# Opening of an attention and feed-forward kernel: constant-tile matmuls during the first loads, bias columns straight from DRAM, x of the first group in halves

## The chip, the cores and the metric

The kernel runs on one core of one Trainium2 chip. The metric is the device time of one execution in microseconds (us), lower is better. A run gives several executions; the profile is that of one.

## The reference, cut to what matters

x is 2 x 4096 x 256, float32. One causal attention layer and one routed feed-forward layer, each followed by a layer norm:

```python
qkv = x @ w_attn + b_attn                       # 256 -> 768
attn = softmax(q @ k.T / sqrt(256) + causal_mask)
x = layernorm(x + (attn @ v) @ w_proj + b_proj)
scores = x @ w_router                            # top 3072 of 4096 rows of a batch
x = layernorm(where(row is among the top, gelu(x @ w_block), x) + x)
```

## The kernel before, in words

The 8192 rows are cut into 16 groups G of 512 rows, 8 for each batch. A group's queries are projected, multiplied with the keys of all its earlier tiles, put through a softmax and multiplied with the values; then come the output, the norm and the feed-forward part. Projection matrices are folded. A = Wq Wk^T serves for the scores, so that "q" is x A plus a column `ucol`, and x itself plays the keys. WV = Wv Wp (less its last column) serves for the values. Every float32 operand of a large product is held as a high part (rounded, written by ScalarE) and a low part (the rest, written by VectorE or GpSimd), and `split3` makes three matmuls of each pair.

The start is the function `prepare`. TensorE makes, in the program's order:
- `columns` (L562): six matmuls of one column that turn the row `b_row` of biases into columns in PSUM, copied to `bcols` (L603).
- `product` (L554): wq times wk, from which VectorE makes A's high and low part (`a_parts`, L597 and L599).
- `sums` (L569, L572, L575): ten matmuls of one column with the biases (`ucol`, the last column of WV, `bqbk`).
- then `pe_q` of group 0 (L498 into fbank from A and xT), twice six matmuls of 512 columns;
- `values_weights` (L580) and `bias` (L586, L587), from which VectorE makes WV (`w_parts`, L615 to L625) and `b_tot`;
- `scores` of group 0 (L498 into sbank), `pe_v` of group 0 (L498 into fbank from WV), and the row maxima (`row_max`, L871 and L892).

In the trace a plain float32 matmul shows as two records (a product's four matmuls are 8 records); L498's are one record each.

x of group 0 goes from DRAM into `xraw` (L667), is rounded by ScalarE (`xhi`, L687) and its low part comes from VectorE for the first 128 channels (`first_xlo`, L696) and from GpSimd for the others (L692). `block_parts` and `router_sum` (L636 to L644) make the feed-forward weights' parts and wait for the loads of w_block and w_router.

The order on each engine is written out ahead of time. Every operation belongs to a named stream of its engine; a planner (`planned`) steps through estimated costs and start times and takes, among the streams' next operations, the one that can start first. `MARGIN_US` makes a stream look later, `PREFER_US` decides between those that can start at once, `COLD_US` is until when TensorE's work is costed at `COLD` = 1.85 times, and `DMA_BYTES_US` is the rate of a load. The engines then run these orders strictly, with semaphore waits. SP issues all DMAs, in its own order. In front of GpSimd's planned order stand the memsets of the constants.

Of the kernel before, what the change touches and what calls it, by code (L numbers as in the profile page):

```python
# [16 lines left out]
P = 128  # L17
# [25 lines left out]
LATE = 2 * (T // GQ) - 2  # L43

# [12 lines left out]
MARGIN_US = {"attention_out router": 3, "project xhi": 2, "final scale": 1.5, "out": 1, "final result": 1,  # L57
             "row_max reduce": 1, "scores hide": 1, "final_roots": 0.6, "values load": 0.6, "ffn aggr": 0.6,
             "project load": 0.3, "proj": 0.3, "ffn flo": 0.3}
# [5 lines left out]
class Rehearsal:  # L65
# [27 lines left out]
    def matmul(self, out, lhs, rhs, start, stop):  # L93
        passes = 4 if rhs.dtype == F32 else 1
        self.time += max(.06, .0132 + self.per_element * passes * out.shape[-1])
        return self
# [96 lines left out]
def planned(todo, signalled, urgent):  # L193
# [23 lines left out]
    for _ in range(sum(len(m) for s in todo.values() for m in s.values())):  # L217
# [28 lines left out]
        if r.bytes:  # L246
            dma = max(when + DMA_US, dma) + r.bytes / DMA_BYTES_US
# [23 lines left out]
def program(nc, x, xt, w_attn_t, b_attn, w_proj, b_proj, w_router, w_block, out):  # L271
# [61 lines left out]
    with ctx:  # L333
# [74 lines left out]
        b_row = ring[0:1, STAGED + 6:STAGED + 8, :].rearrange("p n c -> p (n c)")[:, 0:3 * C]  # L408
# [12 lines left out]
        ld_xt0 = [sem(f"ld_xt0_{n}") for n in range(EARLY + 1)]  # L421
        ld_x = [sem("ld_x0"), sem("ld_x1")]
# [6 lines left out]
        p_a, p_bcols, p_u, p_w, p_btot = sem("p_a"), sem("p_bcols"), sem("p_u"), sem("p_w"), sem("p_btot")  # L429
# [64 lines left out]
        def split3(eng, o, lhs, rhs, chunks):  # L494

            todo = [(lh, rh, k) for k in range(chunks) for lh, rh in ((0, 0), (0, 1), (1, 0))]
            for n, (lh, rh, k) in enumerate(todo):
                mm = eng.matmul(o, lhs(lh, k), rhs(rh, k), start=n == 0, stop=n == len(todo) - 1)  # L498
            return mm
# [25 lines left out]

        def prepare():
# [6 lines left out]
            def load_b(sp):  # L533
                sp.dma_start(b_row, b_attn.rearrange("(a c) -> a c", a=1)).then_inc(ld_b, 16)

            def load_w(sp):
                sp.dma_start(wv_t, wt_rows[2]).then_inc(ld_w, 16)
                sp.dma_start(wp, w_proj.rearrange("(k p) c -> p k c", p=P)).then_inc(ld_w, 16)
                sp.dma_start(bp_row, b_proj.rearrange("(a c) -> a c", a=1)).then_inc(ld_w, 16)

            def load_block(sp):
                sp.dma_start(wb, w_block.rearrange("(k p) c -> p k c", p=P)).then_inc(ld_ffw, 16)
                sp.dma_start(wr[:, :], w_router.rearrange("(a c) -> a c", a=1).broadcast_to([P, C])).then_inc(ld_ffw, 16)
            at("sp", "prepare", load_b)
            at("sp", "prepare", load_qk)
            project_load(0)
# [11 lines left out]
            def columns(pe):  # L558
                pe.wait_ge(ld_b, 16)
                pe.wait_ge(g_const, 1)  # L560
                for n in range(3 * CC):
                    mm = pe.matmul(small[:, n:n + 1], b_row[:, n * P:(n + 1) * P], one_row[:, 0:1], start=True, stop=True)  # L562
                mm.then_inc(p_bcols, 1)

            def sums(pe):
                pe.wait_ge(v_bcols, 2)
                for m in range(CC):
                    for k in range(CC):
                        pe.matmul(small[:, 8 + m:9 + m], wk_t[:, k, m * P:(m + 1) * P], bcols[:, 0, k:k + 1], start=k == 0,  # L569
                                  stop=k == CC - 1)  # L570
                    for k in range(CC):
                        pe.matmul(small[:, 10 + m:11 + m], wq_t[:, k, m * P:(m + 1) * P], bcols[:, 1, k:k + 1],  # L572
                                  start=k == 0, stop=k == CC - 1)
# [4 lines left out]
            def values_weights(pe, m, k):  # L578
                pe.wait_ge(ld_w, 16 * 3)
# [3 lines left out]
            def bias(pe):  # L583
                pe.wait_ge(v_bcols, 3)
# [3 lines left out]
            for op in (columns, product, sums):  # L588
                at("pe", "prepare", op)
            pe_fill["values weights"] = [lambda pe, m=m, k=k: values_weights(pe, m, k) for m in range(CC) for k in range(CC)] + [bias]  # L590
# [10 lines left out]
            def bias_columns(dve):  # L601
                dve.wait_ge(p_bcols, 1)
                dve.tensor_copy(bcols[:, :, :].rearrange("p s k -> p (s k)"), small[:, 0:3 * CC]).then_inc(v_bcols, 1)  # L603
                dve.wait_ge(v_bcols, 1)
# [3 lines left out]
            def bias_sums(dve):  # L608
                dve.wait_ge(p_u, 1)
                dve.tensor_copy(ucol[:, :], small[:, 8:8 + CC]).then_inc(v_u, 1)  # L610
                dve.tensor_copy(bqbk[:, :], small[:, 12:13]).then_inc(v_u, 1)

            def w_parts(dve):
# [6 lines left out]
                dve.wait_ge(p_u, 1)  # L620
                dve.tensor_copy(w_diff[:, :, LAST], small[:, 10:10 + CC]).then_inc(v_wdiff, 1)
                dve.wait_ge(v_wdiff, 2)
                dve.tensor_copy(WV[:, 0], w_diff).then_inc(v_wv, 1)
                dve.wait_ge(v_wv, 1)
# [15 lines left out]
            for op in (bias_columns, bias_sums):  # L640
                at("dve", "prepare bias", op)
# [3 lines left out]
            at("dve", "prepare late", w_parts)  # L645
# [13 lines left out]
        def project_load(G):  # L659
            b, g = groups[G]  # L660

            def load(sp):
                if G == EARLY + 1:
# [4 lines left out]
            at("sp", "project load" if G else "prepare", load)  # L668

        def project(G):  # L670
# [17 lines left out]
            at("act", "project xhi", xhi)  # L688

            def xlo(pool, k):  # L690
                pool.wait_ge(a_xhi, G + 1)
                pool.tensor_tensor(xT[:, 1, k, cols], raw_of(G)[:, k, :], f32(xT[:, 0, k, cols]), ALU.subtract).then_inc(g_xlo, 1)  # L692

            def first_xlo(dve):
                dve.wait_ge(a_xhi, 1)
                dve.tensor_tensor(xT[:, 1, 0, cols], xraw[:, 0, :], f32(xT[:, 0, 0, cols]), ALU.subtract).then_inc(v_xlo, 1)  # L696
            if G == 0:
                at("dve", "prepare xlo", first_xlo)
            for k in range(1 if G == 0 else 0, CC):
                at("pool", "project xlo", lambda pool, k=k: xlo(pool, k))  # L700

            def pe_q(pe, m):
                xlo_made(pe, G)
                if G == 0:
                    pe.wait_ge(v_a, 2)
                freed(pe, ("q", G, m))
                split3(pe, bank_of(("q", G, m))[:, :], lambda h, k: A[:, h, k, m * P:(m + 1) * P],
                       lambda h, k: xT[:, h, k, cols], CC).then_inc(p_proj, 1)
# [268 lines left out]
        def attention_out(G):  # L977
# [5 lines left out]
            def load(sp):  # L983
                if G >= 2:
# [3 lines left out]
                    filled(sp, ("ft", G - 2, 1))  # L988
                sp.dma_start(r, x_rows[b][:, tile0:tile0 + QT, :]).then_inc(ld_x[G % 2], 16)
# [597 lines left out]
        def _(pool):  # L1587

            pool.memset(ones[:, :], 1.0).then_inc(g_const, 1)
# [3 lines left out]
            pool.memset(ones_bf[:, :], 1.0).then_inc(g_const, 1)  # L1593
# [64 lines left out]
```

## Time and profile before

| | us |
|---|---|
| median of 3 runs (990.3 to 991.2) | 990.65 |
| profiled execution | 990.68 |
| its span in the trace | 988.9 |
| TensorE busy | 943.7 |
| VectorE busy | 771.7 |
| ScalarE busy | 637.6 |
| GpSimd busy | 280.0 |

The span runs from the first to the last instruction; 1.8 us of the profiled execution lie outside it. PE is TensorE's matmuls, PEld its weight loads, DVE VectorE, ACT ScalarE, POOL GpSimd, SPq the DMA issues of SyncE. Busy time is a sum over stages: TensorE is nearly always busy from 50 us to 940 us, and has pauses at both ends.

### The profile page before, as it was taken

Reading aid. Unit: us, or ns where it says so; the run is one execution under the profiler, and the core shown is the slowest. Engines: PE = TensorE matmul, PEld = TensorE weight load, DVE = VectorE, ACT = ScalarE, POOL = GpSimd, SP = SyncE. Lnnn points to the kernel's source line nnn. Section 1 sums busy time; section 2 is a strip of 40 time slices with the busy share of each in tenths; the row PEclk is TensorE's granted clock in tenths of the full one; section 3 lists DMA queues with packets and bytes.
Section 4 is the critical chain, followed back from the end, with each engine's and each line's share of the span. In section 5 each row is a group of like instructions: output and inputs, shape, how many; then the busy total and the mean of one; then the engine's idle time right before and its main releaser. Section 6 shows DMA issues by size and latency. Waiting matters only on the chain.

```text
span 988.9 us, 15341 instructions
## 1 busy us (share of the span) xinstructions
PE 943.7 (95%) x4922; PEld 804.9 (81%) x4922; DVE 771.7 (78%) x1475; ACT 637.6 (64%) x1005; POOL 280.0 (28%) x426
## 2 busy tenths in 40 slices
PE   7899999999999999999999999999999999998972
PEld 6788888888888888888888888888788888887851
DVE  4689697966876695679698889888799779469977
ACT  3557576663873595567667757585688558348983
POOL 5421235141041024513343332212101502121323
PEclk9999999999999999999999999999999999999975
DMA  5542445343353336558533334335777434337915
GB/s 195 199 135 75 118 129 160 107 139 107 96 153 114 96 107 188 160 184 267 169 118 118 117 125 142 118 106 190 240 228 241 137 107 123 122 96 242 344 53 171
DMA packets 88948, 149.26 MB, mean 151 GB/s; under 512 B 7586, under 2 KB 25379, under 8 KB 88868
## 3 DMA queue, kind: packets, MB, share of 16 engines
q1 hardware_dynamic: 88868, 148.28, 47.3%
q8 instruction: 40, 0.66, 0.3%
q14 instruction: 40, 0.33, 0.1%
HBM read 108.40 MB, written 39.85 MB: 150 GB/s over the span
## 4 chain that ended last, share of the span: by engine, by line
PE 87%; DVE 4%; ACT 3%; DMA 2%; issue 2%; POOL 1%; DVEq 0%; SPq 0%; ACTq 0%
PE sbank L498 36%; PE fbank L498 12%; PE obank L955 11%; PE obank L957 11%; PE obank L956 11%; DMA xraw<-xt 2%; PE fbank L1034 1%; PE fbank L1174 1%; PE mbank L871 1%; DVE tail L1528 1%; PE mbank L892 1%; ACT parts L916 1%; ACT ring L909 1%; ACT tail L1518 1%; DVE runmax L833 1%
## 5 line engine op out<-in xcount | busy, mean ns | idle before, releaser
L498 PE MATMUL sbank<-qT,xT 128*128 128x512 f32 (+2 forms) x1728 | 410.4, 378 | 4.2 <-issue 2.2
L498 PEld LDWEIGHTS sbank<-qT,xT 128*128 128x128 f32 x1728 | 305.9, 188 | 58.8 <-issue 3.7
L796 ACT COPY ring<-sbank 128x512 f32<-128x512 f32 (+3 forms) x288 | 157.6, 549 | 174.9 <-PE sbank L498 120.1
L955 PE MATMUL obank<-ring_lo,vs 128*128 128x512 f32 (+3 forms) x576 | 219.1, 380 | 3.2 <-ACT ot_sb L1006 1.6
L957 PE MATMUL obank<-parts,vs 128*128 128x512 f32 (+3 forms) x576 | 216.5, 376 | 0.0
L956 PE MATMUL obank<-parts,vs 128*128 128x512 f32 (+3 forms) x576 | 216.3, 376 | 0.0
L921 DVE TENSOR_TENSOR ring_lo<-ring,parts 128x1024 fp32r<-128x1024 f32 (+4 forms) x176 | 176.2, 1011 | 34.3 <-ACT parts L916 33.4
L902 DVE TENSOR_TENSOR ring<-ring,mbank 128x1024 f32<-128x1024 f32 (+4 forms) x176 | 159.8, 949 | 11.1 <-PE mbank L892 11.1
L916 ACT CAST parts<-ring 128x1024 fp32r<-128x1024 f32 (+4 forms) x176 | 145.4, 833 | 34.1 <-PE obank L957 33.6
L838 DVE TENSOR_TENSOR runmax<-ring,runmax 128x1024 f32<-128x1024 f32 x84 | 108.5, 1292 | 69.9 <-ACT ring L796 69.4
L909 ACT ACTIVATE ring<-ring 128x1024 f32<-128x1024 f32 (+4 forms) x176 | 143.5, 844 | 25.3 <-DVE ring L902 25.0
L955 PEld LDWEIGHTS obank<-ring_lo,vs 128*128 128x128 f32 x576 | 108.7, 189 | 21.6 <-ACT parts L916 3.3
L957 PEld LDWEIGHTS obank<-parts,vs 128*128 128x128 f32 x576 | 108.6, 188 | 19.6
L956 PEld LDWEIGHTS obank<-parts,vs 128*128 128x128 f32 x576 | 108.8, 189 | 18.0
L1219 POOL TENSOR_TENSOR yb<-xres,yb 128x512 f32<-128x512 f32 x28 | 36.4, 1321 | 295.2 <-ACT yb L1210 295.2
L998 POOL TENSOR_TENSOR xres<-xres,b_tot 128x512 f32<-128x512 f32 x32 | 50.2, 1591 | 69.8 <-DMA xres<-x 64.8
L692 POOL TENSOR_TENSOR xT<-xraw,xT 128x512 fp32r<-128x512 f32 x27 | 39.1, 1468 | 51.7 <-ACT xT L687 51.7
L498 PE MATMUL fbank<-WV,xT 128*128 128x256 f32 x384 | 51.3, 283 | 1.7 <-DVE WV L625 1.7
L498 PE MATMUL fbank<-xT,A 128*128 128x512 f32 x192 | 51.0, 403 | 1.8 <-DVE A L599 0.9
L498 PEld LDWEIGHTS fbank<-WV,xT 128*128 128x128 f32 x384 | 49.5, 191 | 3.9 <-DVE WV L625 2.2
L833 DVE TENSOR_TENSOR runmax<-ring,runmax 128x512 f32<-128x512 f32 (+3 forms) x76 | 41.7, 548 | 13.5 <-ACT ring L796 11.8
L970 POOL TENSOR_SCALAR roots<-mv_h 128x4 f32<-128x4 f32 x15 | 8.0, 532 | 144.8 <-DVE mv_h L1057 144.8
(190 smaller groups left out, 1013.0 us busy)
## 6 DMA issues: line engine op xcount, KB each, us to landing
vs<-v_scratch SPq DMA_DIRECT2D x288, 256.0 KB, 2.7
v_scratch<-vnew SPq DMA_DIRECT2D x30, 512.0 KB, 3.1
xres<-x SPq DMA_DIRECT2D x16, 512.0 KB, 4.0
out<-tail SPq DMA_DIRECT2D x32, 256.0 KB, 3.3
xraw<-xt SPq DMA_DIRECT2D x14, 512.0 KB, 4.2
x_scratch<-xres SPq DMA_DIRECT2D x14, 512.0 KB, 3.1
y_scratch<-yb SPq DMA_DIRECT2D x14, 512.0 KB, 3.9
tail<-x_scratch SPq DMA_DIRECT2D x28, 256.0 KB, 3.2
```

The costliest lines, as they stand in the source:

```text
L498: mm = eng.matmul(o, lhs(lh, k), rhs(rh, k), start=n == 0, stop=n == len(todo) - 1)
L796: act.copy(slot(n)[:, c0:], sbank[n % NSS][:, c0:]).then_inc(a_copy, 1)
L833: dve.tensor_tensor(runmax[:, 0, c0:], slot(n)[:, c0:], runmax[:, 0, c0:], ALU.max).then_inc(v_max, 1)
L838: dve.tensor_tensor(runmax[:, :, :], slots(ns, 0), runmax[:, :, :], ALU.max).then_inc(v_max, 1)
L902: dve.tensor_tensor(slots(ns, c0), slots(ns, c0), mbank[:, None, c0:].broadcast_to([P, len(ns), GQ - c0]), ALU.subtract).then_inc(v_z, 1)
L909: act.activation(slots(ns, c0), slots(ns, c0), ACT.Exp, scale=SCALE).then_inc(a_exp, 1)
L916: act.copy(hi_of(u), slots(ns, c0)).then_inc(a_hi, 1)
L921: dve.tensor_tensor(slots_lo(ns, c0), slots(ns, c0), f32(hi_of(u)), ALU.subtract).then_inc(v_lo, 1)
L955: pe.matmul(o, vh, lo_, start=i == 0, stop=False)
L956: pe.matmul(o, vh, hi_, start=False, stop=False)
L957: mm = pe.matmul(o, vl, hi_, start=False, stop=last)
L998: pool.tensor_tensor(r[:, 2 * j:2 * j + 2], r[:, 2 * j:2 * j + 2], b_tot[:, None, :].broadcast_to([P, 2, C]), ALU.add).then_inc(g_xres, 1)
```

## The change

- `WARM` = 8 matmuls of `ones_bf` (128 x 128) with 512 columns of the same tile, bfloat16, into obank[1], as TensorE's first work. GpSimd sets `ones_bf` first.
- `columns` and its copy are gone: the host hands b_attn over as 128 x 6, and one DMA puts it into `bcols`. `sums` is cut in three: `key_sums` behind `product`, `query_sums` and `bias_product` behind `values_weights`.
- SP's order at the start: wq, wk, x of group 0 in two halves of 128 channels (256 KB each, their own semaphores), then b_attn. The loads of wv, wp, b_proj wait until the first half of x has landed; those of x of groups 1 and 2 and of the residual's x of groups 0 and 1 wait until wv has landed.
- `first_xhi` rounds the halves one by one. GpSimd makes the low part of half 0, VectorE that of half 1; the wait for the latter stands in front of the fourth matmul of the first query product.
- `block_parts` and `router_sum` stand behind the two `qlo` of group 0 in the stream "project qlo". `w_parts` is cut in three operations.
- The planner's numbers: `COLD_US` 21 to 4, a first load rate, a longer least time of a plain float32 matmul, and many entries of `PREFER_US` and `MARGIN_US`. They bear on the orders of the whole program.

The diff, cut to its core:

```diff
+WARM = 8
-DMA_US, DMA_BYTES_US = 1.6, 320e3
+DMA_US, DMA_BYTES_US, FIRST_BYTES_US = 1.6, 320e3, 250e3
-COLD_US, COLD, COLD_STREAMS = 21.0, 1.85, ("late", "last")
+COLD_US, COLD, COLD_STREAMS = 4.0, 1.85, ("late", "last")
-PREFER_US = {"attention_out stats": 60, "row_max reduce": 60, "project qhi": 60, "scores copy": 30,
-             "softmax hi": 30, "row_max": 8, "scores hide": 8, "project vlo": 8, "softmax lo": 4, "ffn gelu": 4,
-             "ffn aggr": -8, "attention_out router": -8, "final pick": -15, "attention_out score": -30,
-             "softmax z": -30, "project vhi": -30}
+PREFER_US = {"ffn flo": 100, "row_max reduce": 60, "project qhi": 60, "attention_out residual": 60,
+             "project qlo": 60, "attention_out stats": 30, "scores copy": 30, "softmax hi": 30, "final_roots": 30,
+             "row_max": 8, "scores hide": 8, "prepare xlo": 8, "project xhi": 8, "project vlo": 4,
+             "softmax lo": 4, "ffn gelu": 4, "softmax exp": -4, "ffn aggr": -8, "attention_out router": -8,
+             "project vhi": -8, "final pick": -15, "attention_out score": -30, "softmax z": -30,
+             "final result": -30}
...
             def load_b(sp):
-                sp.dma_start(b_row, b_attn.rearrange("(a c) -> a c", a=1)).then_inc(ld_b, 16)
+                sp.dma_start(bcols[:, :, :].rearrange("p s k -> p (s k)"), b_attn).then_inc(ld_b, 16)
+            def load_x(sp, k):
+                sp.dma_start(xraw[:, k, :], xt_rows[0][:, k, 0:GQ]).then_inc(ld_xh[k], 16)
             def load_w(sp):
-                sp.dma_start(wv_t, wt_rows[2]).then_inc(ld_w, 16)
+                sp.wait_ge(ld_xh[0], 16)
+                sp.dma_start(wv_t, wt_rows[2]).then_inc(ld_wv, 16)
...
-            at("sp", "prepare", load_b)
             at("sp", "prepare", load_qk)
-            project_load(0)
+            for k in range(CC):
+                at("sp", "prepare", lambda sp, k=k: load_x(sp, k))
+            at("sp", "prepare", load_b)
             at("sp", "prepare", load_w)
...
+            def warm(pe):
+                pe.wait_ge(g_const, 1)
+                for _ in range(WARM):
+                    pe.matmul(obank[1][:, :].rearrange("p (a b) -> p a b", a=QT), ones_bf[:, :],
+                              ones_bf[:, None, :].broadcast_to([P, QT, P]), start=True, stop=True)
-            for op in (columns, product, sums):
+            for op in (warm, product, key_sums):
                 at("pe", "prepare", op)
+            pe_fill["values weights"] += [lambda pe, m=m: query_sums(pe, m) for m in range(CC)] + [bias_product, bias]
...
             for op in (block_parts, router_sum):
-                at("dve", "prepare block", op)
+                after_queries.append(op)
...
             def load(sp):
+                if G <= EARLY:
+                    sp.wait_ge(ld_wv, 16)
...
+            def first_xhi(act, k):
+                act.wait_ge(ld_xh[k], 16)
+                act.copy(xT[:, 0, k, cols], xraw[:, k, :]).then_inc(a_xhi if k else a_xh0, 1)
...
             def pe_q(pe, m):
-                xlo_made(pe, G)
                 if G == 0:
                     pe.wait_ge(v_a, 2)
+                    pe.wait_ge(g_xlo, 1)
+                else:
+                    xlo_made(pe, G)
                 freed(pe, ("q", G, m))
                 split3(pe, bank_of(("q", G, m))[:, :], lambda h, k: A[:, h, k, m * P:(m + 1) * P],
-                       lambda h, k: xT[:, h, k, cols], CC).then_inc(p_proj, 1)
+                       lambda h, k: xT[:, h, k, cols], CC,
+                       between=(lambda: pe.wait_ge(v_xlo, 1)) if G == 0 and m == 0 else None).then_inc(p_proj, 1)
...
             project(G)
+            if not G:
+                for op in after_queries:
+                    at("dve", "project qlo", op)
```

## Rows read from the trace of the kernel before

**Rows 1.** The page: busy time and share of each engine
```profile
PE 943.7 (95%) x4922; PEld 804.9 (81%) x4922; DVE 771.7 (78%) x1475; ACT 637.6 (64%) x1005; POOL 280.0 (28%) x426
```

**Rows 2.** Stretches: busy time by engine, granted clock, DMA share, GB/s
```profile
0.00:50.00 50.00, 40.82 (x212) 34.81 (x213) 28.64 (x59) 20.37 (x34) 24.55 (x48) 0.97 0.59 197
50.00:940.00 890.00, 880.98 (x4594) 752.89 (x4593) 707.16 (x1295) 588.59 (x912) 241.50 (x349) 1.00 0.48 151
940.00:988.90 48.90, 21.92 (x120) 17.23 (x118) 35.90 (x122) 28.68 (x61) 13.94 (x30) 0.64 0.32 110
```

**Rows 3.** Timeline of PE: start, us, line, instructions, idle before
```profile
2.21 2.71 PE L562 MATMUL mbank<-ones,ring 1*128 1x1 f32 x12 [2.21 <-DMA ring<-b_attn]
4.85 3.41 PE L554 MATMUL sbank<-ring 128*128 128x256 f32 x8
...
11.33 4.50 PE L498 MATMUL fbank<-xT,A 128*128 128x512 f32 x12 [0.94 <-DVE A L599]
15.66 1.89 PE L580 MATMUL obank<-ring 128*128 128x256 f32 x8
...
18.35 0.69 PE L587 MATMUL obank<-ring,ones 1*128 1x256 f32 x2
19.72 1.63 PE L498 MATMUL sbank<-qT,xT 128*128 128x512 f32 x6 [0.68 <-issue]
23.08 3.14 PE L498 MATMUL fbank<-WV,xT 128*128 128x256 f32 x24 [1.74 <-DVE WV L625]
...
28.35 0.89 PE L498 MATMUL sbank<-qT,xT 128*128 128x128 f32 x6 [0.37 <-ACT ring L796]
```

**Rows 4.** Short stretches of the start, same columns as rows 2
```profile
4.85:8.10 3.25, 3.25 (x9) 2.67 (x9) 0.95 (x3) 0.06 (x1) 0.69 (x11) 1.00 0.88 272
8.10:10.40 2.30, 2.29 (x21) 2.20 (x19) 1.28 (x6) 0.99 (x1) 1.23 (x1) 1.00 1.04 384
11.30:15.70 4.40, 4.37 (x13) 3.51 (x14) 0.01 (x1) 2.32 (x3) 3.73 (x4) 0.63 0.99 338
...
29.20:36.40 7.20, 3.96 (x21) 2.74 (x21) 5.45 (x12) 2.83 (x5) 2.19 (x3) 1.00 0.85 292
```

**Rows 5.** Timeline of SP: DMA issues
```profile
0.79 0.35 SPq L534 DMA_DIRECT2D ring<-b_attn  x1
1.19 0.90 SPq L531 DMA_DIRECT2D ring<-w_attn_t  x2
2.14 0.47 SPq L667 DMA_DIRECT2D xraw<-xt  x1
```

**Rows 6.** The view of DMAs: issues, KB each, median us to landing
```profile
ring<-w_attn_t SPq DMA_DIRECT2D x3, 256.0 KB, 3.0
```

**Rows 7.** Timeline of the other engines at the start
```profile
0.78 0.20 POOL L1589 MEMSET ones<- 128x128 f32 x1 [0.29 <-POOLq L1651]
...
8.04 1.04 ACT L687 CAST xT<-xraw 128x1024 fp32r<-128x1024 f32 x1 [5.98 <-DMA xraw<-xt]
...
9.12 0.69 DVE L696 TENSOR_TENSOR xT<-xraw,xT 128x512 fp32r<-128x512 f32 x1 [3.18 <-ACT xT L687]
9.17 1.76 POOL L692 TENSOR_TENSOR xT<-xraw,xT 128x512 fp32r<-128x512 f32 x1 [3.57 <-ACT xT L687]
...
10.49 0.69 DVE L599 TENSOR_TENSOR A<-sbank,A 128x512 fp32r<-128x512 f32 x1
...
15.92 1.33 DVE L636 CAST WB<-ring 128x512 fp32r<-128x512 f32 x1 [4.61 <-DMA wr<-w_router]
...
21.40 1.63 DVE L625 TENSOR_TENSOR WV<-ring,WV 128x512 fp32r<-128x512 f32 x1
```

**Rows 8.** The chain that ended last, start and us
```profile
11.03 7.62 DMA xraw<-xt
...
22.51 3.85 DMA xraw<-xt
```

**Rows 9.** A stretch late in the program, columns of rows 2
```profile
710.00:720.00 10.00, 7.12 (x28) 5.41 (x27) 6.72 (x12) 6.84 (x12) 0.09 (x1) 0.89 0.76 250
```

More of the change, by code:

```diff
@@ L94, in matmul @@
         passes = 4 if rhs.dtype == F32 else 1
-        self.time += max(.06, .0132 + self.per_element * passes * out.shape[-1])
+        self.time += max(.22 if passes == 4 else .06, .0132 + self.per_element * passes * int(np.prod(out.shape[1:])))
         return self
@@ L246, in planned @@
         if r.bytes:
-            dma = max(when + DMA_US, dma) + r.bytes / DMA_BYTES_US
+            dma = max(when + DMA_US, dma) + r.bytes / (DMA_BYTES_US if when > 10 else FIRST_BYTES_US)
         for t, name, by in r.incs:
@@ L524, in program @@
         w_psum = obank[1][:, :].rearrange("p (m c) -> p m c", m=CC)
+        after_queries = []
         def prepare():
@@ L556, in product, with key_sums, query_sums, bias_product @@
                 mm.then_inc(p_a, 1)
-            def columns(pe):
+            def key_sums(pe):
                 pe.wait_ge(ld_b, 16)
[L560 to L566, printed above, removed]
                 for m in range(CC):
                     for k in range(CC):
[L569 to L573, printed above, removed]
+                        mm = pe.matmul(small[:, 8 + m:9 + m], wk_t[:, k, m * P:(m + 1) * P], bcols[:, 0, k:k + 1],
+                                       start=k == 0, stop=k == CC - 1)
+                mm.then_inc(p_u, 1)
+            def query_sums(pe, m):
+                pe.wait_ge(v_u, 1)
+                for k in range(CC):
+                    mm = pe.matmul(small[:, 10 + m:11 + m], wq_t[:, k, m * P:(m + 1) * P], bcols[:, 1, k:k + 1],
+                                   start=k == 0, stop=k == CC - 1)
+                mm.then_inc(p_u, 1)
+            def bias_product(pe):
+                pe.wait_ge(v_bcols, 1)
                 for k in range(CC):
@@ L587, in bias @@
                 pe.matmul(obank[0][:, 0:C], one_row, bp_row, start=False, stop=True).then_inc(p_btot, 1)
-            for op in (columns, product, sums):
+            def warm(pe):
[4 more added lines that the diff above has]
+            for op in (warm, product, key_sums):
                 at("pe", "prepare", op)
-            pe_fill["values weights"] = [lambda pe, m=m, k=k: values_weights(pe, m, k) for m in range(CC) for k in range(CC)] + [bias]
+            pe_fill["values weights"] = [lambda pe, m=m, k=k: values_weights(pe, m, k) for m in range(CC) for k in range(CC)]
+            pe_fill["values weights"] += [lambda pe, m=m: query_sums(pe, m) for m in range(CC)] + [bias_product, bias]
             def a_parts(dve):
@@ L639, in prepare @@
             at("dve", "prepare", a_parts)
-            for op in (bias_columns, bias_sums):
+            at("dve", "prepare keys", key_bias)
+            for op in (bias_columns, row_bias):
                 at("dve", "prepare bias", op)
@@ L687, in xhi @@
                 act.copy(xT[:, 0, :, cols], raw_of(G)).then_inc(a_xhi, 1)
-            at("act", "project xhi", xhi)
+            def first_xhi(act, k):
+                act.wait_ge(ld_xh[k], 16)
+                act.copy(xT[:, 0, k, cols], xraw[:, k, :]).then_inc(a_xhi if k else a_xh0, 1)
+            if G:
+                at("act", "project xhi", xhi)
+            else:
+                for k in range(CC):
+                    at("act", "project xhi", lambda act, k=k: first_xhi(act, k))
             def xlo(pool, k):
-                pool.wait_ge(a_xhi, G + 1)
+                if G:
+                    pool.wait_ge(a_xhi, G + 1)
+                else:
+                    pool.wait_ge(a_xh0, 1)
                 pool.tensor_tensor(xT[:, 1, k, cols], raw_of(G)[:, k, :], f32(xT[:, 0, k, cols]), ALU.subtract).then_inc(g_xlo, 1)
@@ L988, in load @@
                     filled(sp, ("ft", G - 2, 1))
+                else:
+                    sp.wait_ge(ld_wv, 16)
                 sp.dma_start(r, x_rows[b][:, tile0:tile0 + QT, :]).then_inc(ld_x[G % 2], 16)
@@ L1587, in _ @@
         def _(pool):
+            pool.memset(ones_bf[:, :], 1.0).then_inc(g_const, 1)
             pool.memset(ones[:, :], 1.0).then_inc(g_const, 1)
```

48 lines of the change are left out of this document (27 added, 21 removed).

## The prediction

> **What bounds the kernel now.** I read the page's busy shares first: TensorE 95%, VectorE 78% [rows 1]. The reader is to see that no other engine comes near. The table by stretches says where the missing 5% are: from 50 to 940 us TensorE is busy 881.0 of 890 us, in the first 50 us it is 40.8, and in the last 48.9 us 21.9 [rows 2]. The middle is TensorE's own work, which the edit leaves as it is, so whatever brings the middle forward comes off the end, and nothing else at the start does. The last stretch is VectorE's (35.9 of 48.9 us) and its matmuls run at a mean granted clock of 0.64; the edit touches it only through the planner's orders.
>
> So I read the start instruction by instruction on TensorE [rows 3]. It is in a chain there: biases land, `columns`, `product` from 4.85, sums, a pause of 0.94 us for A's low part, queries at 11.33, a pause of 0.68 us before the first scores, 1.74 us before v, 0.37 us at 28.35, and then 7.2 us of which 3.96 are busy [rows 4].
>
> Two stretches run slowly. The product's 8 records take 3.41 us; the same 8 records of the same shape take 1.89 us at 15.66 [rows 3]. That is the ratio of TensorE's two levels, 1.2 and 2.4 GHz, though the clock column reads 1.00 at 4.85 [rows 4]; it seems to show changes only, so at the very start I trust the durations. The queries' 12 matmuls take 4.50 us with 0.63 granted in the stretch [rows 3, 4]; the six score matmuls of the same 512 columns at 19.72 take 1.63 us. Twelve at full clock are then 2.9 us (0.24 each and the last one's latency).
>
> **The first operands.** Before, b_attn's issue stood first (0.79), wq and wk followed at 1.19 and 1.64, the latter landing 3.0 us after its issue, about 4.65 [rows 5, 6]. Now the two issues are 0.40 us earlier: 4.25. The warm matmuls begin when GpSimd's first memset is done, 0.78 + 0.20 = 0.98 us [rows 7]. The trace has no bfloat16 matmul of 512 columns; the nearest are float32r ones of one pass, 0.375 each in the mixed queries and about 0.48 at half clock, so 3.0 to 3.8 us for eight. They end between 4.0 and 4.8; I take 4.6 (nearer the half-clock row, since the engine comes from rest). They can hold the product by up to 0.55 us; beside them `columns` (2.71 us) goes, whose work was hidden before the product anyhow: nothing gained, nothing lost. The product starts at 4.6 instead of 4.85.
>
> At what clock? After 2.7 us of one-column matmuls and 3.4 us of product the sums run fast (20 records in 2.3 us, 0.115 each), so steady activity from 2.2 to 8 had raised it; with dense matmuls from 1 us on I take the product at full clock: 1.9 us, end 6.5 (at half clock 8.0, the upper bound).
>
> The Trainium skill, TensorE: Matmul & The Clock Gate, "What's actually happening", says the same from the other side: rest is the half-rate state, activity releases it, idling gives it back. By its first half the eight matmuls do their work; by its second half the clock could be lost again in the wait ahead of the queries, as it was at 11.33; that outcome is priced as a rival below from the rows alone.
>
> **x and the biases.** x of group 0 was issued at 2.14 and reached ScalarE at 8.04, 5.9 us later, with wv, wp and x of group 1 behind it in the same queue and 272 GB/s moved meanwhile [rows 4, 5, 7]. Now it is issued at 1.7 and 2.15 and nothing but 3 KB follows until half 0 has landed. 512 KB at 272 GB/s are 1.9 us, after wk's 4.25: half 0 at 5.2, half 1 at 6.2. The other end is no gain but the earlier issue: 7.6. ScalarE rounds a half in 0.55 us (1.04 for both): done at 5.8 and 6.8. GpSimd's low part costs up to 1.76: 7.6. VectorE's costs 0.69 and is wanted only by the fourth matmul.
>
> The bias columns are 128 rows of 24 bytes. No row prices this alone; the row of 3 KB landed in time for a start at 2.21, 1.4 us after issue, and here they queue behind x, so 6.3 (up to 7.7, x's upper end). `key_sums` are 8 records: 0.9 us, 6.5 to 7.4 (8.6).
>
> The Trainium skill, DMA: Bandwidth & Descriptors, "Specifications", speaks against such rows: runs under 512 bytes are below the size for line rate and cost a read-modify-write. With 128 of them it would add little even so; no row here shows it, and the sum goes by the bounds above.
>
> A's parts on VectorE: 6.56, two of 0.69, 7.95. So all three inputs of the queries meet at 7.6 to 8.0, and I take 8.0 for their start: **3.3 us earlier** (with x at its upper end and half a clock, 9.3: 2.0 earlier). At full clock they take 2.9 for 4.5 us: **1.6 us**.
>
> **From the queries to the end of group 0's scores.** The pause of 0.68 us goes: VectorE's `qlo` was then queued behind WB's high part, which sat 4.61 us waiting for w_router [rows 7]; it now comes first, and TensorE has the values' weights to do from 10.9 to 15.7. The pause of 1.74 goes too if WV is ready before TensorE has done the rest: it needs p_w, about 12.8, the last column (14.3), the two parts, 0.7 and up to 1.63, so about 17; with block_parts' 2.4 us in front, 20. TensorE's other work (values' weights and bias 15.66 to 19.04, i.e. 3.4; the moved sums 1.4; scores about 4, by 1.63 for the 512 columns at 19.72 and less for 384, 256 and 128) lasts until about 19.7, so at worst 0.3 us of it stays. **2.4 us**. The 0.37 at 28.35 stays. The moved sums are 12 records of 0.115: they were ahead of the queries and now lie on the path behind them, **1.4 us lost**.
>
> Costed at nothing: the second half's own DMA issue (0.45 us of SP) and the waits that now stand ahead of wv's and the later x loads. Queued on SP behind them are w_block, w_router, the residual's x and the x of groups 1 and 2: wv goes out at 5.2, the others when it has landed, about 3 us later, at 8.2. Group 1's x, 512 KB behind wp at some 340 GB/s [rows 4], lands at 11 to 13, and its queries, which came after 28.35 + 0.89, are wanted at about 23. That cover is 10 us; without it the delay would be paid in full. The stretch 29.2 to 36.4 with 3.2 us of pauses is the maxima's chain and I leave it alone (1.5 either way).
>
> **The sum.** -3.3 - 1.6 - 2.4 + 1.4 = -5.9 us on the profiled 990.68, that is 984.8; the median of the runs is 0.03 from it, so 984.8 stands for that too. The changed preferences reorder all engines everywhere. In the middle TensorE has 9 us of pauses to win or lose [rows 2]; I take 0, and 2 us for the gain's end.
>
> **Rivals.**
> - **Half clock all the same** (0.15): the product at 3.4 us and the queries at 4.5 cost 1.5 + 1.6 back: -2.8, 987.9. For it: the clock was lost at 11.33 after a stretch of full PE rows [rows 4], and `key_sums` are as thin. Against: they last 0.9 us, not 2.3.
> - **The loads did not move** (0.17): x of group 3 lands at 18.65 and that of group 4 at 26.36 [rows 8], the first 7.6 us after its issue, behind the other loads in the queue, the second behind group 3's low part. Neither gets 6 us earlier. If an engine's order has the rounding of such an x (or the wait for w_router) ahead of v's evacuation, as now at 26.4, TensorE stands there again. About 3.4 us are given back: 988.2.
> - **Hidden anyway** (0.08): the maxima's chain of group 0 and the first value loads set the date of the middle; 990 to 990.7.
> - **Slower** (0.10): the new orders make one kind of gap more often. At 710 us TensorE is 2.88 us idle, waiting for scores copied late, and the clock falls to 0.89 over 10 us, 1.1 more: 4.0 us a gap [rows 9]. One more leaves 988.8; two end at 992.8. It decides from 7.9 us given back, two gaps; two at the batches' joints would be enough. Against it: in 890 us there is 9 us of pause in all.
>
> The forecast has the remaining 0.50. Its own range is 982.0 to 987.0: reorder gain of 2 us and a later meeting of product and x. Faster by over 0.2% (below 988.7, about what a measurement of this kernel can tell from no change) holds the forecast, half clock, and three quarters of the second rival: 0.77. Within 0.2%: the rest of it, the third, one gap of the fourth: 0.15. Slower: 0.08. The range of 8 in 10 is 981.8 to 989.6: from the bounds' best to the case that one gap or late loads leave 1 us.
>
> **What would show it.** TensorE's queries of group 0 at 8.0 (before 11.33) and in 2.9 us; the product's 8 records in 1.9 us; the first scores at about 15.7 (before 19.72); v of group 0 without a pause over 0.5 us; group 0's last scores (before 28.35) at about 22.5; in the table by stretches 50 to 940 us with the same 9 us of pauses. Wrong would be: 0.5 granted after 8 us; a wait of ScalarE for x of group 3 or 4 ahead of v; VectorE waiting for w_router; TensorE's pauses from 50 us on over 12 us; an end stretch longer than 48.9 us.

## The result and the profile after

| | before | changed |
|---|---|---|
| median of 4 runs, us | 990.92 | 982.74 |
| lowest to highest, us | 990.3 to 991.56 | 982.11 to 984.62 |
| profiled execution, us | 990.68 | 982.49 |
| its span, us | 988.9 | 980.8 |

The ratio of the changed kernel's time to before's is 0.9926, 95% interval 0.9911 to 0.9942: faster by 8.2 us in the medians where 5.9 were forecast, and inside the range of 981.8 to 989.6. Between the profiled executions it is 8.19 us.

The page's busy shares of the changed kernel answer to [rows 1], its stretches to [rows 2] (the cut at 932 keeps the end stretch at the same length):

```profile
PE 941.2 (96%) x4918; PEld 800.3 (82%) x4918; DVE 774.7 (79%) x1474; ACT 638.5 (65%) x1006; POOL 279.4 (28%) x426
```

```profile
0.00:50.00 50.00, 43.42 (x232) 35.10 (x232) 35.41 (x64) 22.54 (x38) 25.33 (x48) 1.00 0.59 197
50.00:932.00 882.00, 875.98 (x4565) 748.24 (x4566) 703.36 (x1289) 586.37 (x907) 239.51 (x346) 1.00 0.48 152
932.00:980.80 48.80, 21.82 (x123) 16.97 (x121) 35.89 (x122) 29.55 (x63) 14.51 (x33) 0.68 0.33 109
```

TensorE has 6.0 us of pauses between 50 and 932 us, before 9.0 between 50 and 940. The end stretch is as long as it was, and TensorE and VectorE are as busy in it.

The changed kernel's timeline of TensorE, against [rows 3] (start, us, line, instructions, idle before):

```profile
1.04 3.53 PE L608 MATMUL obank<-ones_bf 128*128 128x512 bf16 x8 [1.04 <-POOL ones_bf L1639]
4.41 1.90 PE L568 MATMUL sbank<-ring 128*128 128x256 f32 x8
6.35 1.05 PE L576 MATMUL mbank<-bcols,ring 128*128 128x1 f32 x8
7.82 3.01 PE L503 MATMUL fbank<-xT,A 128*128 128x512 f32 x12 [0.41 <-DVE A L622]
...
15.31 2.72 PE L503 MATMUL sbank<-qT,xT 128*128 128x512 f32 x12
18.60 3.13 PE L503 MATMUL fbank<-WV,xT 128*128 128x256 f32 x24 [0.57 <-DVE WV L653]
...
24.44 1.61 PE L503 MATMUL fbank<-xT,A 128*128 128x512 f32 x6 [1.38 <-DVE row_const L805]
...
27.70 1.61 PE L503 MATMUL fbank<-xT,A 128*128 128x512 f32 x6 [1.22 <-DVE qT L766]
...
31.23 1.62 PE L503 MATMUL sbank<-qT,xT 128*128 128x512 f32 x6 [1.49 <-issue]
```

The product's 8 records take 1.90 us (before 3.41), the queries start at 7.82 (11.33) and take 3.01 (4.50), the scores follow at 15.31 (19.72), v at 18.60 (23.08). Then two pauses for VectorE stand that were not there, 1.38 and 1.22 us; the one of 1.76 before the row-max transposes (32.43 before) is gone, that of 1.49 before group 1's scores stays. The other engines of the changed kernel, against [rows 7]:

```profile
5.42 1.36 ACT L722 CAST xT<-xraw 128x512 fp32r<-128x512 f32 x2 [3.35 <-DMA xraw<-xt]
...
6.12 1.27 POOL L734 TENSOR_TENSOR xT<-xraw,xT 128x512 fp32r<-128x512 f32 x1 [0.52 <-ACT xT L722]
...
7.07 0.69 DVE L622 TENSOR_TENSOR A<-sbank,A 128x512 fp32r<-128x512 f32 x1
...
12.80 0.43 DVE L664 CAST WB<-ring 128x512 fp32r<-128x512 f32 x1 [0.46 <-DMA wr<-w_router]
...
16.88 1.66 DVE L653 TENSOR_TENSOR WV<-ring,WV 128x512 fp32r<-128x512 f32 x1
```

ScalarE's first rounding starts at 5.42, not 8.04; it is for half 0 and half 1. A's low part ends last, as forecast. VectorE is at WB from 12.80, and WV's low part ends at 18.54, which is when v starts.

To see where the 8.2 us arise, I cut the executions at four matmuls found in every kernel, and take the distances. M1 is the start of group 1's row-max transposes (55.57 before), M2 a later transpose with a pause of 0.24 us (494.79), M3 the value matmul behind a pause of 1.41 us (904.16), M4 the first feed-forward matmul after the last group's values (943.77). The numbers come from TensorE's timelines.

| us | to M1 | M1 to M2 | M2 to M3 | M3 to M4 | M4 to the end |
|---|---|---|---|---|---|
| before | 55.57 | 439.22 | 409.37 | 39.61 | 45.13 |
| changed | 50.37 | 439.40 | 404.74 | 42.01 | 44.28 |
| difference | -5.2 | +0.2 | -4.6 | +2.4 | -0.9 |

The start gives 5.2 us. Nearly as much again, 4.6, comes between M2 and M3, and half of that is lost behind M3. The pause of 2.35 us at 717 (in the stretch of [rows 9], 2.88 idle and 0.89 granted) is gone, and so is one of 1.09 at 542.

### The profile page after: what moved, and what is told of

Read it like the earlier page. It is cut to its first block, busy times and chain, and to the rows that moved or that the text cites. A ratio compares the mean times of both kernels' runs of the same rounds, so it can differ in the third digit from the quotient of the medians.

```text
span 980.8 us, 15337 instructions
## 1 busy us (share of the span) xinstructions
PE 941.2 (96%) x4918; PEld 800.3 (82%) x4918; DVE 774.7 (79%) x1474; ACT 638.5 (65%) x1006; POOL 279.4 (28%) x426
## 4 chain that ended last, share of the span: by engine, by line
PE 82%; DVE 6%; ACT 4%; issue 3%; DMA 2%; SPq 0%; POOL 0%; DVEq 0%; ACTq 0%
PE sbank L503 35%; PE fbank L503 11%; PE obank L1000 11%; PE obank L1002 11%; PE obank L1001 11%; PE fbank L1221 1%; PE fbank L1081 1%; ACT parts L961 1%; ACT ring L954 1%; DMA out<-tail 1%; DVE tail L1575 1%; PE mbank L916 1%; DMA tail<-y_scratch 1%; DVE runmax L878 1%; PE mbank L937 1%
## 5 line engine op out<-in xcount | busy, mean ns | idle before, releaser
L966 DVE TENSOR_TENSOR ring_lo<-ring,parts 128x1024 fp32r<-128x1024 f32 (+4 forms) x176 | 178.9, 1024 | 31.7 <-ACT parts L961 30.4
L878 DVE TENSOR_TENSOR runmax<-ring,runmax 128x512 f32<-128x512 f32 (+3 forms) x76 | 43.7, 575 | 12.8 <-ACT ring L841 11.1
```

Of the source, the lines that this page charges most:

```text
L878: dve.tensor_tensor(runmax[:, 0, c0:], slot(n)[:, c0:], runmax[:, 0, c0:], ALU.max).then_inc(v_max, 1)
L966: dve.tensor_tensor(slots_lo(ns, c0), slots(ns, c0), f32(hi_of(u)), ALU.subtract).then_inc(v_lo, 1)
```

## The experiments

Each kernel was timed in five rounds beside the kernel before. I give the median time, its ratio to the kernel before with the 95% interval, and M1. Each experiment has one profile, so its M1 is that of one execution.

**Preferences alone.** The kernel before with the changed `PREFER_US` and `MARGIN_US`:

```diff
-PREFER_US = {"attention_out stats": 60, "row_max reduce": 60, ...
+PREFER_US = {"ffn flo": 100, "row_max reduce": 60, ...
-MARGIN_US = {"attention_out router": 3, "project xhi": 2, "final scale": 1.5, ...
+MARGIN_US = {"attention_out router": 3, "final scale": 3, "project xhi": 2, ...
...
```

> The kernel before with only the changed PREFER_US and MARGIN_US. Theory A (the change is two separate gains: about 5.2 us at the start from the loads, the clock and the moved sums, and about 3 us later from the planner's preferences): group 1's row-max transposes stay at 55 to 56 us as before, the gap at 717 us is gone, the time is 986 to 989. Theory B (the later 3 us are chance of where the start's shift lets waits fall): the time is 990 to 992 with the gap at 717 us or one like it. Theory C (the preferences also make the start): transposes of group 1 earlier than 54.

987.16 us, 0.9967 (0.9953 to 0.9982). M1 is at 55.40, as before; M2 to M3 is 404.97, the changed kernel's; M4 to the end is 46.54, that is 1.4 more. The longest wait of TensorE for VectorE between 60 and 930 us in this kernel (total, times, longest):

```profile
PE mbank L873 <- DVE runmax L835: 1.4, 1, 1.4
```

It was 2.4 us at 717 in the kernel before, with the clock's fall behind it; here the clock stays at 1.00 from 700 to 730 us. A pause of 1.37 us at 714 is what is left of it, and the one of 1.09 at 542 is gone. Theory A: the preferences are worth 3 us (medians: 2.9) without any change of M1. Its queries are the slowest of all:

```profile
12.67 5.30 PE L500 MATMUL fbank<-xT,A 128*128 128x512 f32 x12
```

They end at 17.97, 2.1 us later than before (15.83), and M1 is no later. What stands ahead of v on TensorE does not by itself set M1; v waits for VectorE's WV in both kernels.

**All but the preferences.** The changed kernel with the two tables of before:

```diff
-PREFER_US = {"ffn flo": 100, "row_max reduce": 60, ...
+PREFER_US = {"attention_out stats": 60, "row_max reduce": 60, ...
...
```

> The changed kernel with the PREFER_US and MARGIN_US of before; all else as changed. Theory A: group 1's row-max transposes within 0.7 us of the changed kernel's 50.37, a gap of 2 us or more with a fall of the clock between 500 and 890 us, time 985 to 987. Theory B: time within 1 us of the changed kernel's or anywhere else between 981 and 988, not tied to such a gap. Theory C: transposes of group 1 later than 52.

985.19 us, 0.9954 (0.9942 to 0.9966). M1 is at 52.05 and M2 to M3 406.97, which lies between both; there is no gap of 2 us (the largest at that place are 0.97 at 711 and 1.34 at 735) and no fall of the clock between 50 and 940, so theory A is right in the sum and not in the place. Its start:

```profile
4.43 2.90 PE L566 MATMUL sbank<-ring 128*128 128x256 f32 x8
...
9.79 2.50 PE L501 MATMUL fbank<-xT,A 128*128 128x512 f32 x5 [1.67 <-DVE A L620]
```

The product takes 2.90 us after the same eight matmuls. VectorE, in this order, widens the biases before it turns to A (its cast of A at 8.33), so TensorE waits 1.67 us and the queries run slowly. So the order that the preferences make costs the queries a wait. That they have a part in M1 (theory C) is not shown: the changed kernel itself has its M1 at 51.80 in a second profile, below. Relative to the kernel before, this kernel gains 4.8 us and the one above 2.9, together 7.7; the changed kernel itself was 7.7 under before in the series below. The two halves add, as far as such medians tell (the intervals are over 1 us to either side).

**The changed kernel again**, as the measure of the next three.

> The changed kernel as it is, once more, as the measure for the others of this series and to see how much of the start is the same in a second profile. Theory (the product's and the queries' clock at the start is the same in every execution): product's 8 records 1.9 us, queries 3.0 us, group 1's row-max transposes within 0.3 us of 50.37, all times within 1 us. Rival (the clock comes in at another date from execution to execution, as the kernel with the old preferences hints, whose product took 2.90 us after the same eight matmuls): product between 1.9 and 3.4 us and times that spread over 2 us or more.

982.81 us (981.61 to 984.01), 0.9918 (0.9900 to 0.9936). M1 is at 51.80, 1.4 us later than in the first profile; M1 to M2 is 439.34 and M2 to M3 404.94, within 0.2 of the first. TensorE and the others:

```profile
4.43 2.20 PE L568 MATMUL sbank<-ring 128*128 128x256 f32 x8
...
8.19 3.00 PE L503 MATMUL fbank<-xT,A 128*128 128x512 f32 x12 [0.20 <-DVE A L622]
```

```profile
6.07 1.29 ACT L722 CAST xT<-xraw 128x512 fp32r<-128x512 f32 x2 [4.00 <-DMA xraw<-xt]
...
14.79 0.43 DVE L664 CAST WB<-ring 128x512 fp32r<-128x512 f32 x1 [2.09 <-DMA wr<-w_router]
```

The rival holds: the product took 2.20 us, and VectorE waited 2.09 us for w_router where it had waited 0.46. Of the 1.4 us, 0.4 are there when the queries start (8.19 against 7.82) and 0.9 when v does, since WV was made at 19.41 and not at 18.54; the pause for VectorE behind v is 1.87 and not 1.38. Yet the execution lasted 981.61 us, less than the first one: M3 to M4 is 39.66 instead of 42.01. At that place both executions have the same two pauses. Stretches of the first profile of the changed kernel, then of the second:

```profile
710.00:720.00 10.00, 10.00 (x63) 9.00 (x62) 9.35 (x18) 6.55 (x13) 0.00 (x0) 1.00 0.63 201
...
880.00:890.00 10.00, 8.36 (x56) 7.40 (x55) 8.29 (x17) 6.11 (x13) 0.00 (x0) 1.00 0.57 188
890.00:900.00 10.00, 8.47 (x37) 7.07 (x36) 10.00 (x11) 9.83 (x12) 1.31 (x2) 0.83 0.75 246
```

```profile
880.00:890.00 10.00, 8.67 (x62) 7.86 (x60) 7.22 (x15) 5.13 (x11) 0.00 (x0) 1.00 0.42 145
890.00:900.00 10.00, 8.18 (x41) 6.99 (x42) 10.00 (x11) 9.97 (x13) 0.00 (x0) 1.00 0.76 254
```

In the first the clock falls to 0.83 over 10 us after the pauses, in the second it stays. That fall is about 1.6 of the 2.35 us; the rest goes with a pause of 0.46 us at 925 that only the first has (the last section works this out from all profiles). So one execution says little about 2 us.

**No constant-tile matmuls**, orders unchanged (the planner goes on costing them):

```diff
-                for _ in range(WARM):
+                for _ in range(WARM if isinstance(pe, Rehearsal) else 0):
```

> The changed kernel with no constant-tile matmuls; the planner still costs them, so every engine's order is the same. Theory A (they hold the clock up for the product and the queries): the product's 8 records take 3.2 to 3.4 us instead of 1.90, and the queries 3.0 to 4.5; group 1's row-max transposes 1.5 to 3 us later than 50.37, time 984 to 986. Rival (the start is held by loads and by VectorE's queue, so a slow product is absorbed before v): the product is slow but group 1's transposes and the time move by less than 0.7 us.

984.12 us, 0.9933 (0.9918 to 0.9948). M1 at 53.16. TensorE's start:

```profile
4.47 3.75 PE L568 MATMUL sbank<-ring 128*128 128x256 f32 x8 [4.47 <-POOL jtab L1661]
8.02 1.71 PE L576 MATMUL mbank<-bcols,ring 128*128 128x1 f32 x8
```

The product takes 3.75 us and the queries 4.81, both more than I had expected. In the nine profiles with the constant tiles and the same start of the product it takes 3.15 at most. So the constant tiles do give the clock: M1 is 1.4 to 2.8 us later than in the two profiles of the changed kernel. In the time the interval overlaps the changed kernel's, and 1.3 us of medians from two series is no proof.

**The biases as a row again**, in the place of the constant tiles; the bias load is first in the queue again, and the copy of the columns is back:

```diff
-                sp.dma_start(bcols[:, :, :].rearrange("p s k -> p (s k)"), b_attn).then_inc(ld_b, 16)
+                sp.dma_start(b_row, b_line.rearrange("(a c) -> a c", a=1)).then_inc(ld_b, 16)
...
-            for op in (warm, product, key_sums):
+            for op in (columns, product, key_sums):
...
```

> The changed kernel with the biases as a row, turned into columns by six matmuls as before, in the place of the constant-tile matmuls; the bias load is first in the queue again. The prediction's term (these matmuls are hidden ahead of the product; the columns gain nothing but 0.4 us of queue): beside the kernel without constant-tile matmuls, whose product starts at 4.47 and whose group 1 transposes are at 53.16, this one's product starts at 4.8 to 5.0 and its transposes are at 53.0 to 53.8. Rival (the one-column matmuls do warm the clock as well as the constant tile): product in less than 3 us and queries in 3.0 us, transposes near 51.

984.50 us, 0.9934 (0.9916 to 0.9952), M1 at 52.01. The product starts at 5.07 and takes 3.59 us, but the queries, at 10.17, take 3.00. Neither reading is right alone. The one-column matmuls from 2.42 us on do not help the product. That they help the queries is not shown: with the same twelve records from 2.32 us the kernel with the preferences alone had its queries in 5.30 us, and from 2.21 the kernel before in 4.50. The start is no worse than without any matmuls ahead (53.16); the columns by themselves gain nothing that these runs show.

**The loads not held back**, orders unchanged:

```diff
-                sp.wait_ge(ld_xh[0], 16)
+                if isinstance(sp, Rehearsal):
+                    sp.wait_ge(ld_xh[0], 16)
...
-                if G <= EARLY:
+                if G <= EARLY and isinstance(sp, Rehearsal):
                     sp.wait_ge(ld_wv, 16)
...
```

> The changed kernel without the waits that hold back the loads of wv, wp, b_proj until x's first half and of the later x until wv; the planner still counts them, so every order is the same. Theory (x came late because others moved beside it): ScalarE's first rounding at 6.5 to 7.5 us instead of 5.42, the queries at 8.8 to 10 instead of 7.82, but w_router lands earlier and VectorE with it; group 1's row-max transposes between 0.5 and 1.5 us later. Rival (x is short and first in the queue anyway, the waits are worth nothing): rounding before 6, group 1's transposes at 50.4 or earlier.

980.45 us, 0.9895 (0.9875 to 0.9916), M1 at 48.77. In this kernel's timeline:

```profile
6.06 1.31 ACT L723 CAST xT<-xraw 128x512 fp32r<-128x512 f32 x2 [4.00 <-DMA xraw<-xt]
...
12.60 0.42 DVE L665 CAST WB<-ring 128x512 fp32r<-128x512 f32 x1
```

The rival holds, but for 0.06 us in the rounding. x's first half is rounded at 6.06, in the changed kernel's two profiles at 5.42 and 6.07. Over all profiles of x in two loads it is 5.42 to 6.18 with the waits and 5.96 to 6.38 without: what comes behind x in the queue delayed it by no more than it varies. But WB's cast is at 12.60 with no wait, and M1 1.6 to 3.0 us earlier. Once more, beside the combined kernels:

> The kernel without the waits that hold back the loads, once more beside the combined ones. Theory (the waits cost w_router's landing and nothing is won for x): transposes of group 1 within 0.5 us of 48.77, ScalarE's first rounding between 5.4 and 6.2 us as with the waits, time 980 to 981.5, that is 1.5 to 2.5 us under the changed kernel's. Rival (the first profile was a lucky one): transposes at 50 or later, time above 982.

981.78 us, 0.9916 (0.9898 to 0.9932). M1 at 48.88, rounding at 6.15: the start is reproduced. The time is not: M3 to M4 was 42.07 here, with the clock's fall and the pause at 925, and 40.29 in the first, and the median is 1.3 higher. The waits cost the start; that leaving them out makes a faster kernel is not shown.

**The feed-forward weights' parts behind WV:**

```diff
-                after_queries.append(op)
+                at("dve", "prepare late", op)
...
```

> The changed kernel with the feed-forward weights' parts and the router's sum behind the making of WV on VectorE instead of in front of it. Theory (after the queries VectorE's queue is the start's chain: the parts hold it from 12.80 to 14.28 us, WV is done at 18.54 and TensorE stands 0.57, 1.38 and 1.22 us): WV done 1 to 1.5 us earlier, group 1's row-max transposes 1 to 1.5 us earlier than 50.37, time about 981.5 where the later orders are no worse. Rival (the chain is GpSimd's and the loads'): transposes of group 1 within 0.4 us of 50.37.

981.78 us, 0.9915 (0.9901 to 0.9929), M1 at 49.67: 0.7 and 2.1 us before the changed kernel's two. VectorE's timeline of this kernel:

```profile
14.92 0.69 DVE L652 TENSOR_TENSOR WV<-ring,WV 128x512 fp32r<-128x512 f32 x1
...
16.31 0.42 DVE L663 CAST WB<-ring 128x512 fp32r<-128x512 f32 x1
```

WV's low part ends at 15.61, 2.9 us earlier than at 18.54. Of that 0.7 us arrive at M1 of the first profile (2.1 of the second): the planner now has three of the four score products ahead of v, which starts at 19.12 without a pause. M2 to M3 is 406.30, 1.6 more than the changed kernel's. That could be the price of the new orders, but it is not shown. The four kernels that run the changed kernel's own orders with another start (no constant tiles, both without the held-back loads, and x as if in one piece) have 406.07, 406.51, 406.27 and 406.25. So this stretch varies by 1.8 us with the orders as they are, and none of the differences of 2 us in it says what an order is worth.

**Both together**, once with orders planned for it, once with those of the kernel above:

```diff
-                sp.wait_ge(ld_xh[0], 16)
-                if G <= EARLY:
-                    sp.wait_ge(ld_wv, 16)
...
-                after_queries.append(op)
+                at("dve", "prepare late", op)
```

> The changed kernel without the waits that hold back the other loads, as the planner sees it too, and with the feed-forward weights' parts behind WV. Theory (each takes a wait of VectorE's queue off the start: alone 2.0 and 0.7 to 1.4 us): group 1's row-max transposes at 48.3 to 49.3, time 979.5 to 981. Rival (both cure the same wait for w_router, so the second adds nothing, and new orders cost elsewhere): transposes at 48.8 or later, time 980.5 to 982.5.

> The same two edits, but with the orders of the kernel that has only the parts moved (the planner still counts the waits). Theory: start as in the combined kernel, transposes of group 1 at 48.3 to 49.3 us; the time differs from the combined one's only by what 494 to 905 us and the end make of it, under 1.5 us. Rival as for the combined kernel: 48.8 or later.

981.56 us, 0.9911 (0.9886 to 0.9935), M1 at 50.98, after a product of 2.92 us and with the clock at 0.62 from 16 to 20.5 us, where twelve score matmuls took 4.26 us (2.72 in the changed kernel); and 981.69 us, 0.9913 (0.9895 to 0.9932), M1 at 50.02, after wk landed 0.45 us later than elsewhere (product at 4.88). In the times the rival holds: together the edits are no better than either. That both cure the same wait for w_router fits, but these two profiles, each with a late or slow start of its own, do not show it. No kernel here is shown to beat the changed one.

**The query sums ahead of the queries:**

```diff
             for op in (warm, product, key_sums):
                 at("pe", "prepare", op)
+            for m in range(CC):
+                at("pe", "prepare", lambda pe, m=m: query_sums(pe, m))
...
-                dve.wait_ge(p_u, 1)
+                dve.wait_ge(p_u, 1 + CC)
...
```

> The changed kernel with the query sums (8 records of one column) back in front of the queries, the one-column product of the biases left behind. Theory of the prediction (the moved sums lie on the path behind the queries): queries 0.5 us later, what follows 0.4 us earlier, group 1's row-max transposes 0 to 0.5 us earlier. Rival (what holds v is VectorE making WV, and TensorE's sums are hidden in front of it): queries later by 0.4 to 0.9 us, v's start unchanged or later, group 1's transposes 0 to 0.7 us later.

981.77 us, 0.9911 (0.9893 to 0.9929), M1 at 50.47.

```profile
4.43 3.15 PE L568 MATMUL sbank<-ring 128*128 128x256 f32 x8
...
9.11 3.02 PE L503 MATMUL fbank<-xT,A 128*128 128x512 f32 x12
```

Inconclusive. The product took 3.15 us, and the planner moved all scores ahead of v, so that TensorE no longer stood for WV at all. With the queries 0.9 to 1.3 us later, M1 lies between the changed kernel's two.

**x of group 0 as if in one piece:** ScalarE waits for both halves, orders unchanged.

```diff
             def first_xhi(act, k):
+                if not isinstance(act, Rehearsal):
+                    act.wait_ge(ld_xh[1], 16)
```

> The changed kernel, but ScalarE waits for both halves of x before it rounds the first, as if x came in one piece; orders unchanged. Theory (halves matter little, since A's low part ends last before the queries): first rounding 0.6 to 1.0 us later, GpSimd's low part done at 8.5 to 9, queries 0.3 to 1.0 us later, group 1's transposes 0 to 0.7 us later. Rival (the halves carry the start): transposes more than 1 us later than 50.4 to 51.8, the two profiles of the changed kernel.

983.10 us, 0.9924 (0.9903 to 0.9944), M1 at 51.30.

```profile
4.43 2.57 PE L568 MATMUL sbank<-ring 128*128 128x256 f32 x8
...
9.18 3.33 PE L503 MATMUL fbank<-xT,A 128*128 128x512 f32 x7 [1.39 <-POOL xT L736]
```

TensorE waits 1.39 us for GpSimd's low part, and the queries (4.53 us in all) fall to half clock. But the edit did more than it says, as ScalarE's timeline shows:

```profile
5.77 1.28 ACT L724 ACT_TABLE_LOAD   x1 [5.77 <-DMA xraw<-xt]
7.07 1.14 ACT L724 CAST xT<-xraw 128x512 fp32r<-128x512 f32 x2
```

In all other profiles this table load starts at 0.78 or 0.79, while ScalarE has nothing else to do; here the added wait stands ahead of it. Both halves were there at 5.77. Without the 1.28 us GpSimd's low part would end at 7.75 instead of 9.03, A's low part (8.46) would be last, and the queries would start at about 8.5, an estimate from these rows. So nothing here shows that the halves are worth anything. What the run does show is that a start of the queries 1.0 to 1.4 us later, and an end 2.5 to 2.9 us later, need not reach M1, which lies between the changed kernel's two: the pauses of 1.38 and 1.22 us behind v have shrunk to 0.22 and 0.23, with one of 0.76 new between them.

## Why the prediction was right, and where not

- **Bound at the start.** Right. A chain of TensorE, VectorE and the first loads, and what it gives at M1 is there unchanged at M2: M1 to M2 is 439.2 to 439.4 us in all profiles here. But the chain goes by VectorE's WV more than by the queries. With the preferences alone and with x as if in one piece the queries ended over 2 us later and M1 did not.
- **First operands.** Product at 4.6, full clock, 1.9 us: measured 4.41 and 1.90. The eight tiles take 3.53 us, by 4.57 (4.6 forecast). Full clock was one of two bounds and is not certain: after the same tiles the product took from 1.90 to 3.15 us.
- **x.** Half 0 at 5.2: ScalarE starts at 5.42. The reason I gave, that what moved beside it slowed it, is refuted: without the waits x is as early. Its size is not the reason either, as both halves had landed by 7.44 at the latest, and by 5.77 where both are waited for, while the single load of before landed at 8.04. The issue is 0.36 us earlier; what of the rest is due to two loads for one, and what to the biases gone from the front of the queue, no run separates.
- **Queries.** Start at 8.0, 2.9 us: 7.82 and 3.01; 3.3 + 1.6 us forecast, 3.5 + 1.5 found.
- **Pauses behind them.** The pause before the scores went. That for WV fell from 1.74 to 0.57, not to nothing (1.06 in the second profile): WV was done at 18.54, inside my 17 to 20, but the work that was to cover it ended at 18.03 and not at 19.7, since two of the four score products stand behind v. Two pauses for VectorE, 1.38 and 1.22 us, came behind v that I had not counted; 0.37 and 1.76 went. The scores at 15.7: 15.31.
- **Moved sums, 1.4 us lost.** Not borne out: v starts when VectorE has made WV, and the sums lie in front of it on a TensorE that would wait. How much of 1.4 us they cost stays open.
- **Start in all, -5.9.** -5.2 at M1 in the first profile, -3.8 in the second. How it divides among the edits is open but for the constant tiles, 1.4 to 2.8 us at M1. In the time not even they are clear of the noise.
- **The step that failed** is "In the middle TensorE has 9 us of pauses to win or lose; I take 0, and 2 us for the gain's end". The preferences alone gave 2.9 us in the medians. In their one profile M2 to M3 is 4.4 us shorter, the gap at 542 gone and that at 717 down to 1.37 without the clock's fall; the end took 1.4 back. All but the preferences has no gap of 2 us there either (2.4 us shorter), so the gap can close in more than one way. I had the price of such a gap (4.0 us), and used it only for the slower rival. The same row priced a gain.
- **Luck.** The number is near because two errors partly cancel: the start gave 0.7 to 2.1 us less than the 5.9 forecast, and some 3 us came from a term that I had put at nothing.
- **Rivals.** Half clock: absent in the first profile, partly there in others; where the wait ahead of the queries was 1.67 and 1.39 us, they took 4.59 and 4.53 us, as the rival had it. Loads that did not move: there, as VectorE's wait for w_router of 0.46 and 2.09 us, one of the signs that I had named as wrong. Its price at M1 is 0.7 to 3.0 us, by the two kernels that avoid it against the changed kernel's two profiles, and not 3.4. Slower by new gaps: only 0.45 and 0.38 us at 731 and 737 in the changed kernel, though the four kernels with its orders and another start have 1.11 to 1.45 us at 731 to 735; the pauses near 890 us were there before (1.65 and 1.41), and the clock's fall behind them came in one of its two profiles. Hidden: not as a whole, though the queries' part can be.

## What to carry to other kernels

Where an order is written out by estimates, count a change of the estimates as a change of its own, and price both signs: take the largest pauses in the trace, and ask which of them the new order could close. A load held back to speed another must be checked by the other's landing; here x was no earlier and w_router later. An edit that adds a wait can move more than it names: look for every instruction of that engine that now stands behind it. Compare kernels at marks inside the trace before the whole times, when executions differ by 2 us and the edits by 1.

## What the runs showed of the hardware

- The date at which TensorE's clock rises is not that of the program. After the same eight constant tiles from 1.04 us on the product's 8 records took 1.90, 1.96, 2.20 (twice), 2.21, 2.57, 2.90, 2.92 and 3.15 us in the nine profiles in which it could start at 4.4. The Trainium skill, TensorE: Matmul & The Clock Gate, "What's actually happening", says that the switch's date varies by 0.5 us either way, with the phase of a monitor that runs by itself. That the date varies the traces bear out, and by more: the product takes 1.90 us where the clock is up from its start and 3.75 us where it is not up before its end (no constant tiles), so one of 3.15 us had about 2.5 us at half rate, an estimate from these durations. What it depends on no run here shows.
- Two pauses of 1.64 or 1.65 and 1.41 us, 6 us apart, stand near 890 us (898 and 904 before) in all 14 profiles. In four of them the clock fell behind the second (0.83 over 10 us in three), in ten it stayed at 1.00. Without the fall M3 to M4 takes 39.6 to 39.7 us, with it 41.2 to 41.3: 1.6 us. A pause of 0.46 us at 925 to 928, for which the trace names no releaser, stands in four profiles, and 40.4 us with it alone, 42.0 to 42.1 with both: 0.7 to 0.8 us more. (The first kernel with the loads not held back has 40.29, with a wait of 0.19 for a load.)
- The clock column reads 1.00 over the start even where the product runs at half rate; the durations decide there.
- The bias columns, 128 rows of 24 bytes behind x, made TensorE wait 0.31 us in the changed kernel's second profile (`key_sums` at 6.94), and up to 0.56 in the other experiments; in the first `key_sums` started at 6.35, as the product ended.
